# Convolutional window attention on one core: normalisation of queries and keys moved from ScalarE to VectorE, copy of the transposed probabilities moved from VectorE to ScalarE

## The chip, the cores and the metric

The kernel runs on one core of a Trainium2 chip. A core has TensorE (PE), VectorE (DVE), ScalarE (ACT) and GpSimd (POOL), each with its own in-order stream of instructions, a queue for DMA issues on SyncE (SP), and semaphores between them. The metric is the device time of one execution in microseconds (us).

## The reference

The input x is 4 images of 32 channels and 128 by 128 pixels. With gn the normalisation of each channel over its image:

```python
xw = gn(x) cut into 64 windows of 16x16 per image
q, k, v = conv3(xw, qw), conv3(xw, kw), conv3(xw, vw)   # 3x3, then 2x2 pixels into channels:
q, k, v = ln(q), ln(k), ln(v)                            # 64 tokens x 128 features per window, normalised over features
attn = softmax(q @ k.T * SCALE + bias)                   # 8 heads of 16
out  = (attn @ v) @ proj_w.T + proj_b
xr   = xw + out, put back into the image
y    = xr + conv3(gelu(conv3(xr, c1w)), c2w)
return x + y
```

## The kernel before

**Tiling.** Two windows are one pair: 128 tokens on the 128 partitions. An image has 32 pairs. A software pipeline runs over a step number i from -4 to 35; in step i every engine works on other pairs at once. The order on each engine is written out by hand in a function `step` per engine, and every dependence is a semaphore count (`wait_ge`, `then_inc`), so nothing is reordered. Eight steps form a loop body that runs twice; four images run one after the other. Around the change, one step holds:

- TensorE: the query, key and value convolutions of pair i+4 into `y_ps` (L999, L1004), every fourth step the projection into `ox_ps` (L1020), the transposes of queries and keys of pair i+3 into `t_ps` (L1029), the scores of pair i into `s_ps` (L1051), the transpose of the probabilities of pair i-1 into `pt_ps` (L1062, waits for `exped`), the product with the values of pair i-2 into `o_ps` (L1072, waits for `pt_copied`), and one transpose of the output (L986).
- VectorE: statistics of pair i+4 (L547 to L552), scores plus bias `sc` (L558), every fourth step the addition to `xr` (L567), the row maximum `mx` (L573), the copy of `pt_ps` to `pt` (L579), in some steps two memsets of `xnf` (L509, L510), reciprocal `rs` and normalised output `on` of pair i-2 (L587, L593, wait for `pv_done`, the end of L1072).
- GpSimd: the scale `ln_rs` and shift `ln_nr` of the normalisation of pair i+4 (L719 to L726), the subtraction of the maximum from `sc` (L731), the low half `x_lo` of the split input (L701).
- ScalarE: in some steps `xnf` (L766) and the high half `x_hi` (L774), in even steps the affine of queries and keys `q_m`, `k_m` (L816, L820), every fourth step four copies `ot` (L832), then the normalisation of queries and keys of pair i+4 `qk_n` (L845), that of the values `v_bd` (L853), and exp of `sc` of pair i (L861).

I number steps by i modulo 4: the four copies `ot` come in steps 2; L1020, L567, `xnf` and its memsets in steps 3.

**Around the pipeline.** From step 28 on, tiles of the first output convolution (`c1`, L975) take the place of the attention convolutions. The tiles of the second (`c2`, L1094) follow, and the last four of them lie between the steps -4 to -1 of the next image (`head`); there VectorE works off each tile with two instructions in `result` (L609, L614), put behind its own step.

Of the kernel before, what the change touches and what calls it, by code (L numbers as in the profile page):

```python
# [10 lines left out]
ALU = mybir.AluOpType  # L11
# [43 lines left out]
def conv_attention(nc, x_al, x_sh, wqkv, bqkv, bias_t, proj_t, vecs, w1, w2, ident, sel_mean, sel_ones, out):  # L55
    with ExitStack() as ctx:
# [239 lines left out]
        def has(n):  # L296
            return 0 <= n < PAIRS
# [64 lines left out]
        def _(v):  # L362
# [176 lines left out]
            def step(i, p0, h0, r0, rr0, row0, b=None, followed=False):  # L539

                if has(i + 4):
                    m = i + 4
                    v.wait_ge(conv_done, p0 + (m + 1))
                    if m >= 2:
                        v.wait_ge(ln_scales, p0 + (m - 1))
                    for t in range(3):
                        ins = v.bn_stats(ln_st[m % 2][:, t, :], y_ps[m % 2][:, E * t:E * (t + 1)])  # L547
                    ins.then_inc(ln_stats, 1)
                    v.wait_ge(ln_stats, p0 + (m + 1))
                    v.tensor_copy(wait_slot[:, :], vec[:, 0:1])  # L550
                    for t in range(3):
                        ins = v.bn_aggr(ln_mv[m % 2][:, t, :], ln_st[m % 2][:, t, :])  # L552
                    ins.then_inc(ln_moments, 1)
                if has(i):
                    v.wait_ge(scores_done, p0 + (i + 1))
                    if i >= 4:
                        v.wait_ge(ptr_done, p0 + (i - 3))
                    v.tensor_tensor(sc[i % 4][:, :, :, :].rearrange("p (a h) w k -> p a (h w k)", a=2),  # L558
                                    s_ps[:, :, 0:256], biasS[:, :, :], ALU.add).then_inc(biased, 1)

                if i % 4 == 3 and i >= 7:
                    r = (i - 7) // 4
                    v.wait_ge(proj_done, r0 + (r + 1))
                    if i == 7:
                        v.wait_ge(xr_begun, b * 4 + 5)
                    rows = xr[:, bass.ds((row0 + r) * TS, TS), :].rearrange("p i (w j) -> p w i j", w=NWIN)
                    v.tensor_tensor(rows, rows, ox_ps[:, :].rearrange("p (w i j) -> p w i j", w=NWIN, i=TS),  # L567
                                    ALU.add).then_inc(xr_added, 1)
                if has(i):
                    v.wait_ge(biased, p0 + (i + 1))  # L570
                    if i >= 2:
                        v.wait_ge(shifted, p0 + (i - 1))
                    v.tensor_reduce(mx[i % 2][:, :, :], sc[i % 4][:, :, :, :], AX.X, ALU.max).then_inc(maxed, 1)  # L573
                if has(i - 1):
                    m = i - 1
                    v.wait_ge(ptr_done, p0 + (m + 1))
                    if m >= 2:
                        v.wait_ge(pv_done, p0 + (m - 1))
                    v.tensor_copy(pt[m % 2][:, :, :], pt_ps[:, :, :]).then_inc(pt_copied, 1)  # L579

                if i % 4 == 3 and 2 <= (i + 9) // 4 < NROW:
                    row((i + 9) // 4, r0)

                if has(i - 2):
                    m = i - 2
                    v.wait_ge(pv_done, p0 + (m + 1))
                    v.reciprocal(rs[m % 2][:, :, :], o_ps[:, :, :, VW - 1]).then_inc(sums_inv, 1)  # L587
                    v.wait_ge(sums_inv, p0 + (m + 1))
                    if m >= 2:
                        v.wait_ge(ot_done, p0 + (m - 1))  # L590
                    for par in range(2):
                        q = slice(64 * par, 64 * par + 64)
                        ins = v.tensor_tensor(  # L593
                            on[m % 2][q, :, :, :],
                            o_ps[q, :, :, HD * par:HD * (par + 1)].rearrange("p h w d -> p w h d"),
                            rs[m % 2][q, :, :].rearrange("p h w -> p w h").unsqueeze(3).to_broadcast(
                                [64, 2, HP, HD]),
                            ALU.mult)
                    ins.then_inc(normed, 1)

                if PAIRS - 4 <= i < PAIRS and followed:
                    for j in range(2):
                        stats(b + 1, 2 * (i - (PAIRS - 4)) + j)
                for t in low_in.get(i, ()):
                    low(b, t)
# [146 lines left out]
        def _(act):  # L752
# [49 lines left out]
            def step(i, p0, h0, r0, rr0, row0, b=None, followed=False):  # L802
# [7 lines left out]
                if i % 2 == 0 and has(i + 2):  # L810
# [10 lines left out]
                                             ACT.Identity, scale=k_aff[:, par, 0:1], bias=k_aff[:, par, 1:2])  # L821
                    ins.then_inc(qkt_done, 1)

                if i % 4 == 2 and i >= 6:
                    r = (i - 6) // 4
                    act.wait_ge(ot_done, p0 + (4 * r + 4))
                    if r >= 2:
                        act.wait_ge(proj_done, r0 + (r - 1))

                    for w in range(2):  # L830
                        for par in range(2):
                            ins = act.activation(  # L832
                                ot[r % 2][64 * par:64 * par + 64, :].rearrange("p (m w t) -> p m w t", w=2, t=TOK)[:, :, w, :],
                                ox_ps[64 * w:64 * w + 64, :].rearrange("p (m a t) -> p m a t", a=2, t=TOK)[:, :, par, :],
                                ACT.Copy)
                    ins.then_inc(ot_copied, 1)

                if has(i + 4):
                    m = i + 4
                    j = m % 2  # L840
                    act.wait_ge(ln_scales, p0 + (m + 1))
                    if m >= 2:
                        act.wait_ge(tr_done, p0 + (m - 1))
                    for t in range(2):
                        ins = act.activation(qk_n[j][:, t, :].rearrange("p (h y x) -> p h y x", h=HEADS, y=2),  # L845
                                             by_head(y_ps[j][:, E * t:E * (t + 1)]), ACT.Identity,
                                             scale=ln_rs[j][:, t:t + 1], bias=ln_nr[j][:, t:t + 1])
                    ins.then_inc(ln_qk, 1)
                    if m >= 8:
                        act.wait_ge(pv_done, p0 + (m - 7))  # L850
                    for w in range(2):
                        q = slice(64 * w, 64 * w + 64)
                        ins = act.activation(  # L853
                            v_bd[m % 8][q, :, w, 0:2 * HD].rearrange("p h (a y x) -> p h a y x", a=2, y=2),
                            y_ps[j][q, 2 * E:3 * E].rearrange("p (y h a x) -> p h a y x", y=2, h=HP, a=2),
                            ACT.Identity,
                            scale=ln_rs[j][q, 2:3], bias=ln_nr[j][q, 2:3])
                    ins.then_inc(ln_v, 1)
# [375 lines left out]
```

## Time and profile before

| | |
|---|---|
| median of 3 runs | 892.53 us (889.89 to 893.34) |
| profiled execution: time, span | 889.67 us, 887.2 us |
| busy: PE, DVE, ACT, POOL | 86%, 75%, 75%, 57% of the span |
| mean granted TensorE clock | 0.976 of full |

Busy time is the union of an engine's instructions. The profile's averages mix the pipeline's steps with the stages of the two output convolutions, so that a stretch has to be looked at by itself.

### The profile page before, as it was taken

The page shows a single profiled execution, that of the slowest core. Times are in us where ns is not written, and L with a number is a line of the kernel's source. Part 1 is how long each engine was busy: PE and PEld are TensorE (multiplying, and loading weights), DVE is VectorE, ACT ScalarE, POOL GpSimd, SP SyncE. Part 2 cuts the span into 40 slices and gives each one's busy share as a digit, 9 for nine tenths or more (in the row PEclk, how much of TensorE's full clock was granted, in tenths as well). Part 3 has the DMA queues.
Part 4 walks back from the last instruction along what each step waited for, and adds up shares of the span by engine and source line. Part 5 has one row for each costly group of instructions (what it writes and reads, how often), then busy time and mean ns, then how long its engine had stood idle before and what let it go on. Part 6 is the DMA issues. An engine that isn't in the chain of part 4 may idle for free.

```text
span 887.2 us, 19085 instructions
## 1 busy us (share of the span) xinstructions
PE 767.0 (86%) x5704; PEld 540.5 (61%) x5704; DVE 666.9 (75%) x2142; ACT 664.6 (75%) x1351; POOL 506.1 (57%) x857
## 2 busy tenths in 40 slices
PE   0479999999798999999877999998988899999988
PEld 0256776766356777677534767776734576776753
DVE  6557888878656888887675788887876688887575
ACT  1499999765577999976458999986665899997561
POOL 5558777662426777754153777676242667775510
PEclk9989999999998999999999999999998999999999
DMA  6100032000232130300042013020014112000004
GB/s 240 54 28 28 29 121 87 15 1 1 68 121 61 33 118 5 101 1 1 1 155 72 28 29 121 14 88 1 1 54 132 39 54 75 0 1 1 1 1 142
DMA packets 17658, 47.16 MB, mean 53 GB/s; under 512 B 2081, under 2 KB 2721, under 8 KB 17569
## 3 DMA queue, kind: packets, MB, share of 16 engines
q1 hardware_dynamic: 17568, 46.09, 15.9%
q8 instruction: 42, 0.69, 0.3%
q14 instruction: 48, 0.39, 0.1%
HBM read 37.69 MB, written 8.39 MB: 52 GB/s over the span
## 4 chain that ended last, share of the span: by engine, by line
PE 26%; issue 24%; DVE 21%; ACT 16%; POOL 11%; DVEq 1%; DMA 0%; POOLq 0%; SPq 0%; ACTq 0%
PE y_ps L1004 6%; PE s_ps L1094 5%; POOL ln_rs L723 4%; DVE ln_st L547 4%; ACT ot L832 3%; ACT qk_n L845 3%; PE s_ps L1051 3%; PE o_ps L1072 3%; ACT v_bd L853 3%; PE ox_ps L1020 3%; ACT sc L861 2%; ACT q_m L816 2%; PE y_ps L975 2%; PE pt_ps L1062 2%; DVE h_hi L516 2%
## 5 line engine op out<-in xcount | busy, mean ns | idle before, releaser
L845 ACT ACTIVATE qk_n<-y_ps,ln_nr,ln_rs 128x128 f32<-128x128 f32 x256 | 103.3, 455 | 69.0 <-POOL ln_nr L726 67.8
L1004 PE MATMUL y_ps<-w_hi,x_hi 128*128 128x192 f16 (+1 forms) x512 | 151.1, 295 | 0.0
L1004 PE MATMUL y_ps<-w_lo,x_hi 128*128 128x192 f16 (+1 forms) x512 | 150.4, 294 | 0.0
L1004 PE MATMUL y_ps<-w_hi,x_lo 128*128 128x192 f16 (+1 forms) x512 | 150.3, 294 | 0.0
L701 POOL TENSOR_TENSOR x_lo<-xnf,x_hi 128x448 f16<-128x448 f32 (+1 forms) x128 | 140.3, 1112 | 15.1 <-ACT x_hi L774 15.1
L731 POOL TENSOR_TENSOR sc<-sc,mx 128x512 f32<-128x512 f32 x128 | 133.4, 1042 | 22.7 <-DVE mx L573 22.3
L558 DVE TENSOR_TENSOR sc<-s_ps,biasS 128x512 f32<-128x512 f32 x128 | 86.6, 677 | 59.3 <-PE s_ps L1051 57.3
L1072 PE MATMUL o_ps<-v_bd,pt 128*128 128x66 f32 x1024 | 128.6, 268 | 0.0
L547 DVE BATCH_NORM_STATS2 ln_st<-y_ps 128x6 f32<-128x128 f32 x384 | 88.8, 287 | 52.2 <-PE y_ps L1004 44.9
L1072 PEld LDWEIGHTS o_ps<-v_bd,pt 128*128 128x128 f32 x1024 | 124.5, 192 | 0.2
L723 POOL TENSOR_TENSOR ln_rs<-ln_ve,neg_half 128x3 f32<-128x3 f32 x128 | 112.8, 881 | 10.7
L853 ACT ACTIVATE v_bd<-y_ps,ln_nr,ln_rs 64x128 f32<-64x128 f32 x256 | 115.7, 452 | 1.7
L719 POOL TENSOR_TENSOR ln_ve<-ln_mv,eps_y 128x3 f32<-128x3 f32 x128 | 24.6, 192 | 159.8 <-DVE ln_mv L552 158.0
L1062 PE MATMUL pt_ps<-idf,sc 128*128 128x128 f32 x512 | 85.2, 290 | 18.7 <-ACT sc L861 18.4
L861 ACT ACTIVATE sc<-sc 128x512 f32<-128x512 f32 x128 | 80.6, 630 | 26.3 <-POOL sc L731 23.5
L1051 PE MATMUL s_ps<-k_m,q_m 64*128 64x128 f32 x1024 | 93.3, 300 | 1.0 <-issue 0.8
L708 POOL TENSOR_TENSOR xr_lo<-xr,xr_hi 128x512 f16<-128x512 f32 x32 | 36.4, 1138 | 99.7 <-ACT xr_hi L793 99.7
L573 DVE TENSOR_REDUCE mx<-sc 128x8 f32<-128x512 f32 x128 | 87.6, 685 | 4.4
L579 DVE COPY pt<-pt_ps 128x512 f32<-128x512 f32 x128 | 87.2, 681 | 4.5 <-PE pt_ps L1062 4.5
L1051 PEld LDWEIGHTS s_ps<-k_m,q_m 64*128 64x128 f32 x1024 | 68.5, 188 | 26.2 <-issue 26.2
L593 DVE TENSOR_TENSOR on<-o_ps,rs 64x128 f32<-64x128 f32 x256 | 73.9, 289 | 6.2
L1062 PEld LDWEIGHTS pt_ps<-idf,sc 128*128 128x128 f32 x512 | 54.6, 142 | 38.5 <-ACT sc L861 29.4
(160 smaller groups left out, 1619.7 us busy)
## 6 DMA issues: line engine op xcount, KB each, us to landing
xs<-in_x_sh_dram SPq DMA_DIRECT2D x32, 576.0 KB, 3.9
xst<-in_x_al_dram SPq DMA_DIRECT2D x16, 512.0 KB, 7.2
xf<-in_x_al_dram SPq DMA_DIRECT2D x32, 256.0 KB, 4.2
out_dram<-xf SPq DMA_DIRECT2D x32, 256.0 KB, 2.3
wst<-in_wqkv_dram SPq DMA_DIRECT2D x1, 768.0 KB, 3.7
w1s<-in_w_dram SPq DMA_DIRECT2D x1, 256.0 KB, 8.8
w2s<-in_w_dram SPq DMA_DIRECT2D x1, 256.0 KB, 8.8
biasS<-in_bias_t_dram SPq DMA_DIRECT2D x1, 256.0 KB, 9.5
```

Source lines behind the costliest of these rows:

```text
L547: ins = v.bn_stats(ln_st[m % 2][:, t, :], y_ps[m % 2][:, E * t:E * (t + 1)])
L573: v.tensor_reduce(mx[i % 2][:, :, :], sc[i % 4][:, :, :, :], AX.X, ALU.max).then_inc(maxed, 1)
L701: pool.tensor_tensor(at_offset(x_lo[r % 2], a), rows_under(xnf[r % 2], a), at_offset(x_hi[r % 2], a), ALU.subtract).then_inc(xlo_done, 1)
L723: pool.tensor_tensor(ln_rs[j][:, :], ln_ve[j][:, :], neg_half[:, 0:3], ALU.pow).then_inc(ln_pow, 1)
L731: pool.tensor_tensor(sc[i % 4][:, :, :, :], sc[i % 4][:, :, :, :], mx[i % 2][:, :, :].unsqueeze(3).to_broadcast([P, HP, 2, TOK]), ALU.subt ...
L845: ins = act.activation(qk_n[j][:, t, :].rearrange("p (h y x) -> p h y x", h=HEADS, y=2), by_head(y_ps[j][:, E * t:E * (t + 1)]), ACT.Identity,
L853: ins = act.activation(v_bd[m % 8][q, :, w, 0:2 * HD].rearrange("p h (a y x) -> p h a y x", a=2, y=2), y_ps[j][q, 2 * E:3 * E].rearrange(" ...
L861: act.activation(sc[i % 4][:, :, :, :], sc[i % 4][:, :, :, :], ACT.Exp).then_inc(exped, 1)
L1004: ins = pe.matmul(y.rearrange("p (t e) -> p t e", t=3)[:, :, cols], xx[r % 2][:, a, P * s:P * (s + 1)], ww[:, a, :].rearrange("p (t e) -> ...
L1051: ins = pe.matmul(out[:, :, w, :], q_m[h % 2][rows, 2 * (i % 2) + w, :, :].rearrange("p a t -> p (a t)"), k_m[h % 2][rows, :, tok], start= ...
L1062: ins = pe.transpose(pt_ps[:, g, :], sc[m % 4][:, g, :, :].rearrange("p w k -> p (w k)"), idf[:, :])
L1072: ins = pe.matmul(o_ps[:, g, :, :].rearrange("p w d -> p (w d)"), pt[m % 2][:, g, :], v_bd[m % 8][:, g, :, :].rearrange("p w d -> p (w d)" ...
```

## The change

The copy `pt` leaves VectorE and becomes an ACTIVATE Copy on ScalarE, put behind `q_m` and `k_m` and ahead of `ot`. The two `qk_n` instructions leave ScalarE and become tensor_scalar instructions with two per-partition operands on VectorE, put at the end of its step, behind `on`. ScalarE's wait ahead of `v_bd` is now on `ln_qk`, which VectorE raises.

```diff
@@ VectorE, step
                     v.tensor_reduce(mx[i % 2][:, :, :], sc[i % 4][:, :, :, :], AX.X, ALU.max).then_inc(maxed, 1)
-                if has(i - 1):
-                    m = i - 1
-                    v.wait_ge(ptr_done, p0 + (m + 1))
-                    if m >= 2:
-                        v.wait_ge(pv_done, p0 + (m - 1))
-                    v.tensor_copy(pt[m % 2][:, :, :], pt_ps[:, :, :]).then_inc(pt_copied, 1)
-
...
                     ins.then_inc(normed, 1)
 
+                if has(i + 4):
+                    m = i + 4
+                    j = m % 2
+                    v.wait_ge(ln_scales, p0 + (m + 1))
+                    if m >= 2:
+                        v.wait_ge(tr_done, p0 + (m - 1))
+                    for t in range(2):
+                        ins = v.tensor_scalar(qk_n[j][:, t, :].rearrange("p (h y x) -> p h y x", h=HEADS, y=2),
+                                              by_head(y_ps[j][:, E * t:E * (t + 1)]), ln_rs[j][:, t:t + 1],
+                                              ln_nr[j][:, t:t + 1], ALU.mult, ALU.add)
+                    ins.then_inc(ln_qk, 1)
@@ ScalarE, step
                     ins.then_inc(qkt_done, 1)
 
+                if has(i - 1):
+                    m = i - 1
+                    act.wait_ge(ptr_done, p0 + (m + 1))
+                    if m >= 2:
+                        act.wait_ge(pv_done, p0 + (m - 1))
+                    act.activation(pt[m % 2][:, :, :], pt_ps[:, :, :], ACT.Copy).then_inc(pt_copied, 1)
+
...
                     act.wait_ge(ln_scales, p0 + (m + 1))
-                    if m >= 2:
-                        act.wait_ge(tr_done, p0 + (m - 1))
-                    for t in range(2):
-                        ins = act.activation(qk_n[j][:, t, :].rearrange("p (h y x) -> p h y x", h=HEADS, y=2),
-                                             by_head(y_ps[j][:, E * t:E * (t + 1)]), ACT.Identity,
-                                             scale=ln_rs[j][:, t:t + 1], bias=ln_nr[j][:, t:t + 1])
-                    ins.then_inc(ln_qk, 1)
+                    act.wait_ge(ln_qk, p0 + (m + 1))
```

The rows below are ScalarE's instructions from `x_hi` of a step 2 to exp of the same step, before the change; `REGISTER_ALU` prepares a count to wait for.

```order
L774 ACTIVATE x_hi<-xnf 128x8x56
L816 ACTIVATE q_m<-t_ps,q_aff 128x4x64 x2
L820 ACTIVATE k_m<-t_ps,k_aff 128x256 x2
L832 ACTIVATE ot<-ox_ps 64x4x64 x4
L841 REGISTER_ALU
L845 ACTIVATE qk_n<-y_ps,ln_nr,ln_rs 128x128 x2
L850 REGISTER_ALU
L853 ACTIVATE v_bd<-y_ps,ln_nr,ln_rs 64x4x32 x2
L861 ACTIVATE sc<-sc 128x512
```

The same place of the changed kernel:

```order
L779 ACTIVATE x_hi<-xnf 128x8x56
L821 ACTIVATE q_m<-t_ps,q_aff 128x4x64 x2
L825 ACTIVATE k_m<-t_ps,k_aff 128x256 x2
L834 ACTIVATE pt<-pt_ps 128x512
L844 ACTIVATE ot<-ox_ps 64x4x64 x4
L853 REGISTER_ALU
L859 ACTIVATE v_bd<-y_ps,ln_nr,ln_rs 64x4x32 x2
L866 REGISTER_ALU
L867 ACTIVATE sc<-sc 128x512
```

One instruction of 512 elements a partition stands where the four copies begin, and two of 128 are gone ahead of `v_bd`.

The next rows are VectorE's step 3 of the first group of an image (where L567 is still absent), before the change.

```order
L547 BN_STATS ln_st<-y_ps 128x6 x3
L550 COPY wait_slot<-vec 128x1
L552 BN_AGGR ln_mv<-ln_st 128x2 x3
L558 TENSOR_TENSOR sc<-s_ps,biasS 128x512
L573 TENSOR_REDUCE mx<-sc 128x8
L579 COPY pt<-pt_ps 128x512
L507 ISA
L509 MEMSET xnf 32x8x16
L510 MEMSET xnf 32x8x16
L587 RECIPROCAL rs<-o_ps 128x8
L593 TENSOR_TENSOR on<-o_ps,rs 64x128 x2
```

The same step of the changed kernel:

```order
L547 BN_STATS ln_st<-y_ps 128x6 x3
L550 COPY wait_slot<-vec 128x1
L552 BN_AGGR ln_mv<-ln_st 128x2 x3
L558 TENSOR_TENSOR sc<-s_ps,biasS 128x512
L573 TENSOR_REDUCE mx<-sc 128x8
L507 ISA
L509 MEMSET xnf 32x8x16
L510 MEMSET xnf 32x8x16
L580 RECIPROCAL rs<-o_ps 128x8
L586 TENSOR_TENSOR on<-o_ps,rs 64x128 x2
L601 TENSOR_SCALAR qk_n<-y_ps,ln_rs,ln_nr 128x128 x2
```

The copy is gone from the middle, and `qk_n` is the last thing in the step, behind `on`.

## Rows read from the trace of the kernel before

**Rows 1.** The page: busy time, share of the span and instructions per engine.

```profile
PE 767.0 (86%) x5704; PEld 540.5 (61%) x5704; DVE 666.9 (75%) x2142; ACT 664.6 (75%) x1351; POOL 506.1 (57%) x857
```

**Rows 2.** Windows: length, busy PE, PEld, DVE, ACT, POOL, granted clock, DMA share, GB/s.

```profile
300.15:356.65 56.50, 52.96 (x438) 40.34 (x439) 46.68 (x165) 52.18 (x112) 42.03 (x73) 1.00 0.18 59
```

**Rows 3.** Timeline of ScalarE: start, duration, instructions, [idle before and its releaser].

```profile
323.12 0.92 ACT L853 ACTIVATE v_bd<-y_ps,ln_nr,ln_rs 64x128 f32<-64x128 f32 x2
324.06 0.63 ACT L861 ACTIVATE sc<-sc 128x512 f32<-128x512 f32 x1
...
327.94 0.81 ACT L845 ACTIVATE qk_n<-y_ps,ln_nr,ln_rs 128x128 f32<-128x128 f32 x2 [0.81 <-POOL ln_nr L726]
...
331.70 0.81 ACT L845 ACTIVATE qk_n<-y_ps,ln_nr,ln_rs 128x128 f32<-128x128 f32 x2 [0.45 <-POOL ln_nr L726]
...
333.88 0.56 ACT L774 ACTIVATE x_hi<-xnf 128x448 f16<-128x448 f32 x1
...
336.28 1.54 ACT L832 ACTIVATE ot<-ox_ps 64x256 f32<-64x256 f32 x4
337.85 0.81 ACT L845 ACTIVATE qk_n<-y_ps,ln_nr,ln_rs 128x128 f32<-128x128 f32 x2
...
341.38 0.81 ACT L845 ACTIVATE qk_n<-y_ps,ln_nr,ln_rs 128x128 f32<-128x128 f32 x2
```

**Rows 4.** Timeline of a step 3: the projection on PE, then VectorE.

```profile
318.92 1.13 PE L1020 MATMUL ox_ps<-ot,projg 128*128 128x512 f32 x2 [0.33 <-ACT ot L832]
...
320.95 0.69 DVE L558 TENSOR_TENSOR sc<-s_ps,biasS 128x512 f32<-128x512 f32 x1 [1.22 <-PE s_ps L1051]
...
322.15 0.68 DVE L573 TENSOR_REDUCE mx<-sc 128x8 f32<-128x512 f32 x1
...
323.50 0.17 DVE L509 MEMSET xnf<- 32x128 f32 x1
...
324.02 0.21 DVE L587 RECIPROCAL rs<-o_ps 128x8 f32<-128x8 f32 x1
324.27 0.59 DVE L593 TENSOR_TENSOR on<-o_ps,rs 64x128 f32<-64x128 f32 x2
324.93 0.69 DVE L547 BATCH_NORM_STATS2 ln_st<-y_ps 128x6 f32<-128x128 f32 x3
```

**Rows 5.** Timeline of PE: transpose of the probabilities, product with the values.

```profile
340.17 0.66 PE L1062 MATMUL pt_ps<-idf,sc 128*128 128x128 f32 x4 [0.31 <-ACT sc L861]
340.67 1.00 PE L1072 MATMUL o_ps<-v_bd,pt 128*128 128x66 f32 x8
```

**Rows 6.** Groups by line: busy us, mean ns, idle before.

```profile
L547 DVE BATCH_NORM_STATS2 ln_st<-y_ps 128x6 f32<-128x128 f32 x384 | 88.8, 287 | 52.2 <-PE y_ps L1004 44.9 <-issue 4.8
L579 DVE COPY pt<-pt_ps 128x512 f32<-128x512 f32 x128 | 87.2, 681 | 4.5 <-PE pt_ps L1062 4.5
L845 ACT ACTIVATE qk_n<-y_ps,ln_nr,ln_rs 128x128 f32<-128x128 f32 x256 | 103.3, 455 | 69.0 <-POOL ln_nr L726 67.8
L832 ACT ACTIVATE ot<-ox_ps 64x256 f32<-64x256 f32 x128 | 48.3, 377 | 15.9 <-PE ox_ps L986 14.8
L456 DVE TENSOR_SCALAR pbias<-pt_ps,vec,up 128x1 f32<-128x1 f32 x1 | 0.3, 273 | 0.0
```

**Rows 7.** Timeline of ScalarE: `qk_n` in step 2 and in step 26 of an image.

```profile
280.63 0.81 ACT L845 ACTIVATE qk_n<-y_ps,ln_nr,ln_rs 128x128 f32<-128x128 f32 x2 [0.34 <-POOL ln_nr L726]
...
394.18 0.81 ACT L845 ACTIVATE qk_n<-y_ps,ln_nr,ln_rs 128x128 f32<-128x128 f32 x2
```

**Rows 8.** Timeline of a step of the head: GpSimd's last normalisation instruction, VectorE's `result`.

```profile
252.76 0.19 POOL L726 TENSOR_TENSOR ln_nr<-ln_nm,ln_rs 128x3 f32<-128x3 f32 x1
252.99 0.75 DVE L609 SCALAR_TENSOR_TENSOR yt<-s_ps,c_scale,xr 128x512 f32<-128x512 f32 x1 [1.75 <-PE s_ps L1094]
```

**Rows 9.** Timeline of PE behind its longest wait of that stretch.

```profile
271.65 0.68 PE L1029 MATMUL t_ps<-idf,qk_n 128*128 128x128 f32 x2 [3.14 <-ACT qk_n L845]
...
273.42 1.11 PE L1062 MATMUL pt_ps<-idf,sc 128*128 128x128 f32 x4
```

## Prediction

> **What bounds the kernel now.** I first read the busy shares [rows 1]: no engine is full, so the average says nothing and I went to a stretch of the pipeline. Over three groups of four steps, 56.50 us, PE is busy 52.96 and ScalarE 52.18 us at full clock [rows 2]: a group takes 18.83 us, of which PE needs 17.65 and ScalarE 17.39. Then I read ScalarE's timeline. The starts of `qk_n` at 327.94 (a step 0), 331.70, 337.85 and 341.38 give 3.76 us to step 1, 6.15 to step 2, 3.53 to step 3 and, as the group is 18.83, 5.39 to the next step 0 [rows 3]. ScalarE waits 0.81 and 0.45 us per group for GpSimd's `ln_nr`, and else runs through [rows 3]. So ScalarE bounds the kernel, PE 7% behind it. What matters for the change is that the short steps make up for the long one: while ScalarE works on step 2, the other engines go ahead, and the next steps cost less than 4 us.
>
> **What the change adds and removes.**
>
> ScalarE loses two `qk_n`, 0.81 us as a pair [rows 3]; since they overlap by 0.10 (2 x 0.455 against 0.81) [rows 3, 6], the next instruction comes 0.70 earlier. It gains one Copy of 512 elements from PSUM. From below: `ot`, the same function from PSUM for half the elements, 0.377 [rows 6]. From above: twice that, 0.754. Exp has the copy's length and, like it, no per-partition operands: 0.63 [rows 3]. I take 0.60, near exp, which it is most like. Less the overlap, and with 0.02 for its wait, it adds 0.52. ScalarE's own work falls by about 0.2 us a step. Taken alone, that is a gain.
>
> VectorE loses a copy of 681 ns, worth 0.60 in its queue: L573 starts at 322.15, and without the copy the memset could start at 322.90 in place of 323.50 [rows 4, 6]. It gains two tensor_scalar instructions of 128 elements from PSUM with two per-partition operands. The trace has no such row. From below: a statistics instruction of 128 elements from PSUM without such operands, 287 ns. From above: one with two such operands and 1 element, 273 ns [rows 6], all of it fixed, plus 127 elements at what the copy pays per element at most (681/512 = 1.33 ns), 169: 442 ns. I take 0.405, near the top, because the 1-element row has the same operands and everything it takes is fixed; the statistics row less its fixed share gives some 0.13 for the elements. As a pair, less an overlap of 0.08 (three statistics instructions of 0.287 take 0.69 [rows 4, 6]), 0.73. VectorE's work grows by 0.1 us a step; it is busy 46.68 of 56.50 us, 17% idle [rows 2], so this is not the cost.
>
> A rule would make it cheaper. The Trainium skill ("VectorE: DVE Perf Modes", The TRN2 errata) gives 120 cycles plus one per element at 0.96 GHz for VectorE from PSUM: 258 ns for 128, a pair 0.44. By it the forecast below would be 21 us lower (0.29 in 18 steps of each image). For the copy it gives 658 against 681 in the trace, but its fixed share is 125 ns, and the row with two operands has 273. The rows decide.
>
> **The cost is the order.** Now `v_bd` of a pair waits for `qk_n` on VectorE; `qk_n` stands behind `on` of an earlier pair, which waits for L1072; L1072 stands behind L1062, which waits for exp; and exp stands behind `v_bd` on ScalarE. That is a closed ring once per step: queued behind the waiting `v_bd` is exp, and for it wait PE, then VectorE, then ScalarE again. Its links: `v_bd` start to exp start 0.94, exp 0.63 [rows 3]; to L1062 0.05 (taken), from its start to the start of L1072 0.50, L1072 1.00 [rows 5]; to `rs` 0.05 (taken); `rs` start to `on` end 0.84; to the next instruction 0.07 [rows 4]; `qk_n` 0.73; to ScalarE 0.03 (taken from the gap between 337.82 and 337.85 [rows 3]). Sum 4.84 us. The steps of 3.76 and 3.53 us are no longer possible.
>
> Let V be the start of `v_bd` in a step.
> - Step 0 to 1, and 3 to 0: the ring, 4.84 each. In step 0, ScalarE's own work (1.57 for `v_bd` and exp, `x_hi`, four affines, copy) is 1.57 + 2.40 (333.88 to 336.28) + 0.52 = 4.5 [rows 3], hidden.
> - Step 1 to 2: ScalarE's own queue. 6.15 less 0.70 plus 0.52 = 5.97. The ring is shorter and hidden.
> - Step 2 to 3: L1020 waits for `ot`, which ends at V (L1020 at 318.92). From there 2.03 us to L558, through L567, L573, memsets, `rs` and `on` to 324.86, 5.94 us [rows 4]; less 0.60 for the copy, plus 0.07 and `qk_n` 0.73, plus 0.03: 6.17. On this path VectorE was hidden before, because `qk_n` did not wait for it.
>
> A group: 4.84 + 4.84 + 5.97 + 6.17 = 21.82 against 18.83, +2.99 us.
>
> Per image: step 6 to 22 are four such groups, +12.0. The first, from step 2 at 280.63 to step 6 at about 300.1 (the window of [rows 2] begins with the L1020 behind that step), 19.5 us, is without L567 and so without the long step 3: 3 x 4.84 + 5.97 = 20.5, +1.0. The last ends at 394.18 and begins at 300.1 and four groups of 18.83, 375.4 [rows 2, 7]: 18.8 us. It has L567 but no memsets, so its step 3 is 6.17 less about 0.65 (0.52 from the first memset to `rs` and the gap ahead [rows 4]); with two rings and 5.97 it is 21.2, +2.4. The steps on either side I put at +0.8, one late `qk_n`. Sum 16.2, times 4: 64.8 us.
>
> In the head, VectorE now waits for GpSimd inside its step, ahead of `result`. `ln_nr` ends at 252.95, so `qk_n` runs to 253.7, and `result` starts there and not at 252.99, 0.7 later [rows 8]. VectorE was idle for 1.75 there; with 0.7 more per step over it, it becomes the bound. About 1.6 us per head (three steps, less what the last hides), 3 heads: 5.
>
> At steps 28 to 32 there is no `qk_n`, VectorE loses 0.60 a step and PE has the `c1` tiles. If VectorE alone bounds there, 5 steps of 4 images give 12 us back; if PE does, nothing. I count nothing, since ScalarE's copy comes into the way from `pt_ps` to `o_ps`, and keep the 12 for the range.
>
> Sum: 64.8 + 5 = 70 us. On the profiled time of 889.67 that is 960; the median of the runs shown is 2.86 higher, so **962 us**, 7.9% slower.
>
> **The rivals.**
>
> *Only the long places cost.* If PE were ready early and the ring of the light steps had shorter links (`qk_n` as a pair 0.5, no gaps), the two ring steps would be near PE's own (17.65 - 1.13) / 4 = 4.1 [rows 2, 4], and a group 4.1 + 4.1 + 5.97 + 5.94 = 20.1, +1.3: 24 groups and the heads, 36 us, 929 us. For it: a sum of ten links, three of them taken (0.13 us). Against: each other link is in the rows.
>
> *Faster.* ScalarE bounds the kernel and gets lighter. If `qk_n` were always ready when ScalarE comes to `v_bd`, PE would be the bound with 17.65 a group, 1.18 less, 24 groups: 28 us, 864 us. It decides at the point at which step 2 to 3 and the two rings together cost 3.0 us less than I sum, so that the group is 18.83 again; that is a full microsecond off each. It would need `qk_n` to be done before `on`, which the order of VectorE's instructions excludes.
>
> *No change.* The ring just about fills the slack: 21.82 less 3.0 by errors of several links. Same point; 892 us.
>
> *The clock falls.* After an idle time of 3.14 us, PE's L1062 took 1.11 us in place of 0.66 [rows 9, 5], the lower of the two levels (1.2 for 2.4 GHz). With the change PE is busy 17.65 of 21.82 us; the 4.2 idle lie in four steps, about 1 us each. If that sufficed to put a third of a step's 4.4 us of work at the lower level in each group, +1.5 us in each of 24 groups, 36 us: 998 us. That takes an idle time of about 1 us to do what 3.14 did, and I think it unlikely. The Trainium skill ("TensorE: Matmul & The Clock Gate", What's actually happening) also has the clock fall after idle time; by that rule, the row agrees.
>
> **How the numbers follow.** Forecast 0.63, only the long places 0.14, clock 0.09, faster 0.09, no change 0.05. The forecast's own range is 940 to 985: `qk_n` from 0.49 to 0.80 as a pair in three of four steps (-19 to +6 us over 80 steps), latencies of 0.1 us in as many (8 us), ScalarE's copy at 0.38 to 0.75 us in 24 steps (5 and 4 us), the 12 us of steps 28 to 32. To hold 8 in 10 it reaches into both neighbours: 922 to 995. Half a per cent is about what a measurement of this kernel can tell from no change: faster 0.09, same 0.05, slower 0.86.
>
> **What would show it.** Right: ScalarE waits ahead of `v_bd`, put down to VectorE's `qk_n`, in steps 3, 0 and 1 and not in 2; PE waits for exp ahead of L1062 by about 0.5 us more in each of these; the four-step group is near 21.8, ScalarE near 75% busy in it; the pair `qk_n` 0.73, the copy 0.59 us; granted clock 1.00 there; `result` in the head 0.7 later. Wrong: a group below 18.8, or ScalarE without waits ahead of `v_bd`; a group that is long because PE's matmuls are; or time that goes to steps 28 and later.

## The result and the profile after

| | before | after |
|---|---|---|
| median | 892.93 us (889.89 to 896.02, 4 runs) | 969.84 us (968.82 to 970.42, 4 runs) |
| profiled execution: time, span, clock | 889.67, 887.2, 0.976 | 970.42, 968.6, 0.971 |

The ratio is 1.086 (95% interval 1.0821 to 1.0899): 8.6% slower. The forecast of 962 us was 8 us low, and the time lies in the narrower of the two ranges stated with it (940 to 985 us).

The page's busy shares, to be held against [rows 1], with the pair of groups for the two moved operations against [rows 6]:

```profile
PE 784.5 (81%) x5704; PEld 548.2 (57%) x5704; DVE 691.5 (71%) x2270; ACT 647.0 (67%) x1223; POOL 508.4 (52%) x857
```

Groups by line (busy us, mean ns, idle before):

```profile
L601 DVE TENSOR_SCALAR qk_n<-y_ps,ln_rs,ln_nr 128x128 f32<-128x128 f32 x256 | 93.3, 406 | 31.8 <-POOL ln_nr L731 28.5
L834 ACT ACTIVATE pt<-pt_ps 128x512 f32<-128x512 f32 x128 | 77.0, 601 | 20.5 <-PE pt_ps L1068 18.9
```

ScalarE has 17.6 us less work than before and VectorE 24.6 us more, and neither number explains 77 us. The window of one group (length, busy PE, PEld, DVE, ACT, POOL, clock, DMA share, GB/s), against [rows 2]:

```profile
330.93:352.78 21.85, 18.10 (x147) 13.51 (x147) 16.51 (x60) 16.80 (x33) 14.24 (x24) 1.00 0.10 29
```

A group that took 18.83 us takes 21.85, at full clock, and no engine is busy for more than 83% of it. ScalarE was at 92%, now it is at 77%. What bounds the kernel now is a chain of waits that closes on itself (the ring of the prediction), as the rows below and then the experiments show. ScalarE's timeline of the same group shows where it stands still (start, duration, [idle before and releaser]), against [rows 3]:

```profile
330.93 0.93 ACT L859 ACTIVATE v_bd<-y_ps,ln_nr,ln_rs 64x128 f32<-64x128 f32 x2 [2.77 <-issue]
...
335.78 0.93 ACT L859 ACTIVATE v_bd<-y_ps,ln_nr,ln_rs 64x128 f32<-64x128 f32 x2 [0.35 <-issue]
336.73 0.63 ACT L867 ACTIVATE sc<-sc 128x512 f32<-128x512 f32 x1
...
340.63 0.93 ACT L859 ACTIVATE v_bd<-y_ps,ln_nr,ln_rs 64x128 f32<-64x128 f32 x2 [1.61 <-issue]
...
345.00 1.55 ACT L844 ACTIVATE ot<-ox_ps 64x256 f32<-64x256 f32 x4
346.57 0.93 ACT L859 ACTIVATE v_bd<-y_ps,ln_nr,ln_rs 64x128 f32<-64x128 f32 x2
...
352.78 0.46 ACT L859 ACTIVATE v_bd<-y_ps,ln_nr,ln_rs 64x128 f32<-64x128 f32 x1 [2.77 <-issue]
```

`v_bd` waits in step 3 (330.93), 0, 1 and again 3, and not in step 2 (346.57), where the four `ot` copies lie ahead of it. The releaser reads "issue" or `qk_n`, as the profile puts it down; that it is `qk_n` each time is seen from VectorE's rows, which end just before (below, the one at 339.81 ends at 340.54, `v_bd` starts at 340.63). The steps are 4.85, 4.85, 5.94 and 6.21. The rest of the ring in step 0 to 1, on PE and VectorE:

```profile
337.41 0.66 PE L1068 MATMUL pt_ps<-idf,sc 128*128 128x128 f32 x4 [0.51 <-ACT sc L867]
337.90 1.00 PE L1078 MATMUL o_ps<-v_bd,pt 128*128 128x66 f32 x8
...
338.95 0.21 DVE L580 RECIPROCAL rs<-o_ps 128x8 f32<-128x8 f32 x1 [0.58 <-PE o_ps L1078]
339.19 0.59 DVE L586 TENSOR_TENSOR on<-o_ps,rs 64x128 f32<-64x128 f32 x2
339.81 0.73 DVE L601 TENSOR_SCALAR qk_n<-y_ps,ln_rs,ln_nr 128x128 f32<-128x128 f32 x2
...
346.60 1.13 PE L1026 MATMUL ox_ps<-ot,projg 128*128 128x512 f32 x2 [1.08 <-ACT ot L844]
...
348.63 0.69 DVE L558 TENSOR_TENSOR sc<-s_ps,biasS 128x512 f32<-128x512 f32 x1 [1.98 <-PE s_ps L1057]
```

From `v_bd` at 335.78: 0.95 to exp, 0.68 to L1068, 0.49 to L1078, 1.05 to `rs`, 0.86 to `qk_n`, 0.82 to the next `v_bd` at 340.63: 4.85. The last two rows are the long step: `ot` releases L1026 at 346.60, and VectorE's queue from 348.63 on ends with `qk_n`, which releases `v_bd` at 352.78. The waits over the whole run say the same (who waited for what: us in total, times, longest):

```profile
ACT v_bd L859 <- issue: 81.9, 47, 2.8
ACT v_bd L859 <- DVE qk_n L601: 74.8, 54, 3.0
DVE rs L580 <- PE o_ps L1078: 55.6, 79, 3.6
PE pt_ps L1068 <- ACT sc L867: 44.3, 80, 0.9
PE t_ps L1035 <- DVE qk_n L601: 43.5, 39, 5.5
```

Each neighbour in the ring waits for the one ahead of it; in the kernel before the third of these rows had 0.2 us, the fourth 18.4.

**Where the 80.75 us between the two profiled executions lie** (970.42 - 889.67), by the starts of `v_bd` in the 32 steps of each image:

| stretch | forecast, 4 images | measured | per image |
|---|---|---|---|
| steps 6 to 22, four groups | 48 | 55.3 | 14.7, 13.3, 14.8, 12.4 |
| steps 2 to 6 | 4 | 7.0 | 2.2, 1.5, 1.7, 1.6 |
| steps 22 to 26 | 9.6 | 10.1 | 2.5 each |
| all else: head, edges, steps 27 and later | 8.2 | 8.4 | |

The 12.4 of image 4 are groups without disturbance. Images 1, 2 and 3 hold five steps (two, one and two) in which PE ran at the lower of its two clock levels (1.2 for 2.4 GHz), as these rows of PE in image 1 show:

```profile
112.78 1.12 PE L1026 MATMUL ox_ps<-ot,projg 128*128 128x512 f32 x2 [1.08 <-ACT ot L844]
...
118.94 0.44 PE L1035 MATMUL t_ps<-idf,qk_n 128*128 128x128 f32 x2 [1.10 <-DVE qk_n L601]
...
120.68 1.09 PE L1068 MATMUL pt_ps<-idf,sc 128*128 128x128 f32 x4 [0.54 <-ACT sc L867]
121.57 1.81 PE L1078 MATMUL o_ps<-v_bd,pt 128*128 128x66 f32 x8
```

L1068 takes 1.09 us in place of 0.66 and L1078 1.81 in place of 1.00, behind waits of 1.10 and 0.54 us. L1068 and L1078 are links of the ring, so two steps there took 6.20 and 6.09 us in place of 5.00 and 4.85. DMA traffic was high in this place (the DMA engines were busy all the time from 120 to 126), but is not the cause: in image 3 the clock (the third number from the end) was at the lower level with no DMA at all (the second):

```profile
608.82:615.00 6.18, 6.18 (x28) 4.89 (x28) 2.48 (x8) 4.53 (x10) 2.97 (x4) 0.50 0.00 0
```

### The profile page after: what moved, and what is told of

Same layout as the page of the kernel before. It is cut to its first block, busy times and chain, and to the rows that moved or that the text cites. A ratio compares the mean times of both kernels' runs of the same rounds, so it can differ in the third digit from the quotient of the medians.

```text
span 968.6 us, 19193 instructions
## 1 busy us (share of the span) xinstructions
PE 784.5 (81%) x5704; PEld 548.2 (57%) x5704; DVE 691.5 (71%) x2270; ACT 647.0 (67%) x1223; POOL 508.4 (52%) x857
## 4 chain that ended last, share of the span: by engine, by line
issue 31%; PE 27%; DVE 19%; ACT 14%; POOL 7%; DVEq 1%; ACTq 0%; DMA 0%; SPq 0%; POOLq 0%
PE o_ps L1078 7%; PE pt_ps L1068 5%; ACT sc L867 5%; ACT v_bd L859 4%; DVE qk_n L601 4%; PE ox_ps L1026 3%; PE s_ps L1057 3%; POOL ln_rs L728 3%; PE y_ps L1010 2%; PE y_ps L981 2%; ACT ot L844 2%; PE s_ps L1100 2%; DVE yt L614 2%; DVE ln_st L547 2%; DVE h_hi L516 2%
## 5 line engine op out<-in xcount | busy, mean ns | idle before, releaser
L1078 PE MATMUL o_ps<-v_bd,pt 128*128 128x66 f32 x1024 | 131.1, 272 | 0.0
L1078 PEld LDWEIGHTS o_ps<-v_bd,pt 128*128 128x128 f32 x1024 | 127.1, 195 | 0.2
L1068 PE MATMUL pt_ps<-idf,sc 128*128 128x128 f32 x512 | 86.3, 293 | 44.4 <-ACT sc L867 44.3
L601 DVE TENSOR_SCALAR qk_n<-y_ps,ln_rs,ln_nr 128x128 f32<-128x128 f32 x256 | 93.3, 406 | 31.8 <-POOL ln_nr L731 28.5
L1068 PEld LDWEIGHTS pt_ps<-idf,sc 128*128 128x128 f32 x512 | 55.5, 144 | 65.4 <-ACT sc L867 52.3
L1035 PE MATMUL t_ps<-idf,qk_n 128*128 128x128 f32 x256 | 55.5, 299 | 44.7 <-DVE qk_n L601 43.5
L834 ACT ACTIVATE pt<-pt_ps 128x512 f32<-128x512 f32 x128 | 77.0, 601 | 20.5 <-PE pt_ps L1068 18.9
```

Of the source, the lines that this page charges most:

```text
L601: ins = v.tensor_scalar(qk_n[j][:, t, :].rearrange("p (h y x) -> p h y x", h=HEADS, y=2), by_head(y_ps[j][:, E * t:E * (t + 1)]), ln_rs[j] ...
L1068: ins = pe.transpose(pt_ps[:, g, :], sc[m % 4][:, g, :, :].rearrange("p w k -> p (w k)"), idf[:, :])
L1078: ins = pe.matmul(o_ps[:, g, :, :].rearrange("p w d -> p (w d)"), pt[m % 2][:, g, :], v_bd[m % 8][:, g, :, :].rearrange("p w d -> p (w d)" ...
```

## The experiments

All times stand beside the kernel before on the same chip: 891.4 us for the two halves and the two single reorderings, 891.2 for both reorderings, `qk_n` twice, PE's waits filled and `ot` split, 894.3 for the copy twice and for before with exp first. The copy twice, `ot` split and before with exp first are medians of four runs; the other seven have one run each. The kernel before and the kernel after spread by 6.1 and 1.6 us over their four runs, so differences between single runs of a few us say little by themselves. The table gives the time between starts of `v_bd`, the median of each kind of step in the steps 6 to 22 of four images, and the mean length of a group. For the kernel after, 3 to 0 is 4.85 inside a loop body and 5.0 where one begins or ends (4.85 at the end in image 4).

| kernel | us | 3 to 0 | 0 to 1 | 1 to 2 | 2 to 3 | mean group | clock |
|---|---|---|---|---|---|---|---|
| before | 892.9 | 5.34 | 3.76 | 6.14 | 3.53 | 18.83 | 0.976 |
| after | 969.8 | 5.00 | 4.85 | 5.94 | 6.21 | 22.28 | 0.971 |
| only `qk_n` moved | 990.1 | 5.36 | 5.21 | 5.46 | 6.81 | 23.29 | 0.952 |
| only the copy moved | 909.1 | 5.04 | 3.83 | 6.62 | 4.01 | 19.50 | 0.979 |
| after, `qk_n` ahead of `rs` | 922.3 | 5.06 | 4.34 | 5.94 | 4.66 | 20.05 | 0.970 |
| after, exp ahead of `v_bd` | 928.1 | 4.36 | 4.42 | 6.05 | 5.55 | 20.43 | 0.980 |
| both reorderings | 933.5 | 4.81 | 4.37 | 6.06 | 4.98 | 20.54 | 0.966 |
| after, `qk_n` twice | 1033.9 | 5.63 | 5.48 | 5.93 | 6.84 | 24.00 | 0.963 |
| after, copy twice | 986.7 | 4.92 | 4.85 | 6.41 | 6.21 | 22.71 | 0.973 |
| after, PE's waits filled | 964.1 | 4.86 | 4.85 | 5.94 | 6.21 | 21.92 | 0.977 |
| before, `ot` split | 897.9 | 5.97 | 3.75 | 5.36 | 4.04 | 19.13 | 0.977 |
| before, exp first | 1007.8 | 5.20 | 5.28 | 6.29 | 5.75 | 22.68 | 0.966 |

### One half at a time

The first kernel is the changed one with the copy back on VectorE, the second the changed one with `qk_n` back on ScalarE. In short, from after:

```diff
@@ e1_qk_only: VectorE, behind mx
+                if has(i - 1):
...
+                    v.tensor_copy(pt[m % 2][:, :, :], pt_ps[:, :, :]).then_inc(pt_copied, 1)
@@ ScalarE
-                if has(i - 1):
...
-                    act.activation(pt[m % 2][:, :, :], pt_ps[:, :, :], ACT.Copy).then_inc(pt_copied, 1)
```

```diff
@@ e2_copy_only: VectorE, end of step
-                        ins = v.tensor_scalar(qk_n[j][:, t, :].rearrange("p (h y x) -> p h y x", h=HEADS, y=2),
...
@@ ScalarE, ahead of v_bd
-                    act.wait_ge(ln_qk, p0 + (m + 1))
...
+                        ins = act.activation(qk_n[j][:, t, :].rearrange("p (h y x) -> p h y x", h=HEADS, y=2),
+                                             by_head(y_ps[j][:, E * t:E * (t + 1)]), ACT.Identity,
+                                             scale=ln_rs[j][:, t:t + 1], bias=ln_nr[j][:, t:t + 1])
```

> Only the normalisation of queries and keys is on VectorE, behind the normalised output; the copy of the transposed probabilities stays on VectorE. Ring theory: the ring v_bd, exp, transpose, product, normalised output, qk_n is untouched by where the copy is, so two steps stay at 4.85 to 4.95 us; step 1 to 2 falls to 5.45 (ScalarE without the copy), step 2 to 3 rises to 6.8 (VectorE with it): group about 22.0 us, time 965 to 980 us, mid 972. Rival (the cost of the change is ScalarE's copy, which puts exp and the values later): without it the group falls to about 20 us and the time to 930 us or less.

> Only the copy of the transposed probabilities is on ScalarE; the normalisation of queries and keys stays there too. Ring theory: no ring, but ScalarE, which bounds the kernel, gets 0.52 us more per step, 2.08 per group, of which its waits of 1.26 for GpSimd take up a part: group 19.5 to 20.7 us, time 905 to 938 us, mid 919. The two halves then do not add up to the whole (about 80 and 27 against 77). Rival (the copy is what costs): the time is within 15 us of the changed kernel, 955 us or more.

Measured: 990.08 and 909.13. The move of `qk_n` alone makes the ring and costs more than the whole change; the copy alone costs 18 us. In its undisturbed groups the first kernel shows 4.85, 4.84, 5.46 and 6.81, which is 21.96 as said. It is 10 us above its expected range since it has many more steps at the lower clock. PE in one of them, its long wait in step 3 to 0 and what came behind:

```profile
360.45 0.44 PE L1035 MATMUL t_ps<-idf,qk_n 128*128 128x128 f32 x2 [1.70 <-DVE qk_n L608]
...
360.93 1.08 PE L1057 MATMUL s_ps<-k_m,q_m 64*128 64x128 f32 x8
362.19 1.11 PE L1068 MATMUL pt_ps<-idf,sc 128*128 128x128 f32 x4 [0.18 <-ACT sc L867]
```

The two kernels give ScalarE's two terms apart: step 1 to 2 goes from 6.14 to 5.46 without `qk_n` (0.68; the working had 0.70), and from 6.14 to 6.62 with the copy (0.48; it had 0.52). Both together are 5.94, which is what after shows. VectorE's copy costs 0.60 in step 2 to 3 (6.81 against 6.21), as taken.

### Opening the ring by order

If the ring is what costs, the same instructions in another order must give most of it back. One kernel puts `qk_n` directly behind the row maximum, so that it no longer stands behind `on`; the other puts exp ahead of `v_bd`, so that exp no longer stands behind the wait for `qk_n`; the third does both.

```diff
@@ e3_qk_ahead: VectorE, step
                     v.tensor_reduce(mx[i % 2][:, :, :], sc[i % 4][:, :, :, :], AX.X, ALU.max).then_inc(maxed, 1)
+                    for t in range(2):
+                        ins = v.tensor_scalar(qk_n[j][:, t, :].rearrange("p (h y x) -> p h y x", h=HEADS, y=2),
...
                 if i % 4 == 3 and 2 <= (i + 9) // 4 < NROW:
                     row((i + 9) // 4, r0)
...
-                    for t in range(2):
-                        ins = v.tensor_scalar(qk_n[j][:, t, :].rearrange("p (h y x) -> p h y x", h=HEADS, y=2),
@@ e4_exp_first: ScalarE, step, ahead of v_bd
+                if has(i):
+                    act.wait_ge(shifted, p0 + (i + 1))
+                    act.activation(sc[i % 4][:, :, :, :], sc[i % 4][:, :, :, :], ACT.Exp).then_inc(exped, 1)
...
-                if has(i):
-                    act.wait_ge(shifted, p0 + (i + 1))
-                    act.activation(sc[i % 4][:, :, :, :], sc[i % 4][:, :, :, :], ACT.Exp).then_inc(exped, 1)
```

> The changed kernel with qk_n on VectorE moved ahead of the xnf memsets, reciprocal and normalised output, directly behind the row maximum. Nothing else. Ring theory: qk_n no longer waits for the product with the values, the ring is open; what is left is VectorE's own queue (statistics 1.1, wait for GpSimd's scales 1.74, qk_n 0.75, output 0.87: 4.45 us a step), ScalarE's step 1 to 2 of 5.95, step 2 to 3 of 4.75 and step 3 to 0 of 5.15: group about 20.3 us, time 915 to 940 us, mid 928. Rival (VectorE's instructions with two per-partition operands, or its load, are the cost, wherever they stand): the time stays above 960 us.

> The changed kernel with exp put ahead of v_bd on ScalarE; qk_n stays at the end of VectorE's step. Ring theory: exp no longer stands behind the waiting v_bd, so the ring is open at another place; the next one is product, normalised output, qk_n, transposes, scores, transpose of the probabilities, about 4.3 us. Step 2 to 3 keeps its 6.2, step 1 to 2 falls to 5.4: group about 20.1 us, time 915 to 945 us, mid 930. Rival (what costs is that qk_n itself comes late, for the transposes behind it): the time stays above 960 us.

> Both orders changed: qk_n directly behind the row maximum on VectorE, and exp ahead of v_bd on ScalarE. If each only opened the same ring, the second adds little: group 19.4 to 20.0 us, time 905 to 922 us. If ScalarE's step 1 to 2 (5.94 to 6.05) and step 2 to 3 are what is left, the group stays above the 18.83 of the kernel before, and so does the time, by 1% or more. Rival (the two delays are independent and add): 885 us or less.

Measured: 922.31, 928.08 and 933.52. Each single reordering takes back 40 to 48 of the 77 us without moving a single operation to another engine. In the first, `qk_n` stands ahead of `rs`, and the ring steps are shorter. VectorE and ScalarE of its step 3 to 0:

```profile
334.58 0.72 DVE L581 TENSOR_SCALAR qk_n<-y_ps,ln_rs,ln_nr 128x128 f32<-128x128 f32 x2
335.38 0.92 ACT L859 ACTIVATE v_bd<-y_ps,ln_nr,ln_rs 64x128 f32<-64x128 f32 x2 [1.23 <-issue]
...
335.90 0.21 DVE L592 RECIPROCAL rs<-o_ps 128x8 f32<-128x8 f32 x1
```

In the second, the time came as expected and two of the steps did not: step 1 to 2 was to fall to 5.4 and is 6.05, step 2 to 3 was to keep 6.2 and is 5.55. Exp now stands between `ot` and `v_bd`, so step 1 to 2 still holds it, and the long path from `ot` has only its last 5.55 us behind `v_bd`.

That both together give more, which I expected (905 to 922), is refuted: they are slower than the first alone. With exp ahead, `v_bd` comes later in step 2 to 3 (4.98 against 4.66), since exp waits for GpSimd's subtraction, and PE waits longer for `ot`, as it comes to L1025 earlier:

```profile
356.97 1.12 PE L1025 MATMUL ox_ps<-ot,projg 128*128 128x512 f32 x2 [1.92 <-ACT ot L844]
...
362.05 0.63 ACT L852 ACTIVATE sc<-sc 128x512 f32<-128x512 f32 x1 [1.52 <-POOL sc L736]
```

Three steps 2 to 3 are at the lower clock (6.50, 6.52 and 6.40 in place of 4.98). Of the 11 us by which both together are slower than the first, these are 4.5, the order in the groups of steps 6 to 22 is about 3 (an undisturbed group is 20.21 against 20.01); the rest lies outside those groups and was not taken apart.

### Doubling one operation

```diff
@@ e5_qk_twice: VectorE, end of step
+                    for t in range(2):
+                        v.tensor_scalar(qk_x[j][:, t, :].rearrange("p (h y x) -> p h y x", h=HEADS, y=2),
+                                        by_head(y_ps[j][:, E * t:E * (t + 1)]), ln_rs[j][:, t:t + 1],
+                                        ln_nr[j][:, t:t + 1], ALU.mult, ALU.add)
@@ e6_copy_twice: ScalarE
+                    act.activation(pt_x[m % 2][:, :, :], pt_ps[:, :, :], ACT.Copy)
```

> The changed kernel with the two qk_n instructions issued twice on VectorE, once into a tile that nobody reads; 0.65 us more per step there. Ring theory: every step that the ring or VectorE's queue decides gets 0.65 us more (3 to 0 and 0 to 1: 4.85 to 5.5; 2 to 3: 6.21 to 6.86), step 1 to 2 stays at 5.94, since ScalarE's queue decides it and the ring, 5.5, is below: group plus 1.95, four images with 18 such steps each plus 47 us, head and edges plus 8: 1025 us, 1015 to 1040 with more or fewer stretches at the lower clock. Rival (VectorE has a quarter of its time idle, its load hides): within 10 us of the changed kernel, 960 to 980.

> The changed kernel with the copy of the transposed probabilities issued twice on ScalarE, the first time into a tile that nobody reads: 0.52 us more in ScalarE's queue per step. My account of the changed kernel: the copy is not a link of the ring, so the step 1 to 2 (ScalarE's own queue) grows from 5.94 to 6.46, the step 3 to 0, whose ScalarE queue I put at 4.5 us, from 4.85 to about 5.0, and 0 to 1 and 2 to 3 stay; the group goes from 21.85 to 22.5, and the time from 970 to 986 us (979 to 994). Rival: ScalarE's load is paid in every step, 2.1 us a group: 1020 us or more. Rival: the copy is hidden everywhere: 970 us.

Measured: 1033.92, and 986.72 (985.70 to 988.57; ratio to before 1.1052, 1.1007 to 1.1096). A second pair on VectorE is 0.63 to 0.65 in its queue, and exactly the three steps that pass through `qk_n` grow by it: 4.85 to 5.48, 4.85 to 5.48 and 6.21 to 6.84. The step 1 to 2 does not move. A second copy on ScalarE does the reverse: only step 1 to 2 grows, 5.94 to 6.41. Step 3 to 0 stays at 4.85 inside a loop body and 5.0 at its edges, where I had expected it to grow to about 5.0; the median of 4.92 lies between the two, and the steps above 5.0 are again at the lower clock. ScalarE around that step:

```profile
349.30 0.61 ACT L835 ACTIVATE pt_x<-pt_ps 128x512 f32<-128x512 f32 x1
349.78 0.62 ACT L836 ACTIVATE pt<-pt_ps 128x512 f32<-128x512 f32 x1
350.25 1.55 ACT L846 ACTIVATE ot<-ox_ps 64x256 f32<-64x256 f32 x4
351.83 0.92 ACT L861 ACTIVATE v_bd<-y_ps,ln_nr,ln_rs 64x128 f32<-64x128 f32 x2
```

The second instruction moves what follows by 0.48 (349.30 to 349.78), and `v_bd` at 351.83 has no wait to hide it. The two kernels tell the links of the ring from the work beside it.

### The clock

```diff
@@ e8_pe_warm: TensorE, ahead of L1026 in steps 3 and ahead of L1035 in steps 0, for 4 <= i < 28
+                    pe.wait_ge(biased, p0 + i)
+                    for d in range(8):
+                        pe.matmul(s_ps[:, 0, 256:512], w_hi[:, 0, 0:P], w_lo[:, 0, 0:256], start=True, stop=True)
```

> The changed kernel with eight f16 matmuls of 256 columns, 0.86 us, from constants into unused columns of s_ps in each of PE's two longest waits of a group (ahead of L1020 in step 3, ahead of the transposes in step 0), steps 4 to 27. If the single steps of 6.1 us in place of 4.85 come from the lower clock, and this from PE's waits, they vanish: all steps 3 to 0 and 0 to 1 of the middle groups at 4.85 to 5.0, time 960 to 965 us. Rival (they come from elsewhere, or the added matmuls delay PE): the same number of such steps, or 970 us and more.

Measured: 964.09. PE gets work that nobody reads in its two longest waits of a group, and in the steps 6 to 22 none is left that is longer than its kind is at full clock. The group is 21.92 on average against 22.28. A group's window:

```profile
330.00:352.00 22.00, 19.90 (x164) 15.02 (x162) 16.51 (x59) 16.96 (x34) 14.30 (x26) 1.00 0.11 29
```

PE has 1.8 us more to do in a group than in the changed kernel and the kernel is 5.8 us faster. So the clock is worth about 6 us of the 77, and order and queues the rest. That is one run, and counted from the kernel before on its own chip (72.9 us against 76.9) it is 4; the groups themselves, 0.36 us each in 16, give 6.

### Was there a gain in the kernel before?

If ScalarE bounded the kernel before, taking work from its longest step must help. The first kernel does that without touching `qk_n`: two of the four `ot` copies go to VectorE, behind `on`. The second, the kernel before with the same edit of exp as above (ahead of `qk_n` and `v_bd`), is the control for that reordering.

```diff
@@ e7_split_ot (on before): ScalarE, steps 2
-                    for w in range(2):
+                    for w in range(1):
@@ VectorE, steps 2, behind on
...
+                    for par in range(2):
+                        ins = v.tensor_copy(
+                            ot[r % 2][64 * par:64 * par + 64, :].rearrange("p (m w t) -> p m w t", w=2, t=TOK)[:, :, 1, :],
+                            ox_ps[64:128, :].rearrange("p (m a t) -> p m a t", a=2, t=TOK)[:, :, par, :])
...
@@ TensorE, ahead of L1020
-                    pe.wait_ge(ot_copied, r0 + (r + 1))
+                    pe.wait_ge(ot_copied, r0 * 2 + (2 * r + 2))
```

> The kernel before with two of the four ot copies of each step 2 (those of the second window, 64 partitions x 256 elements) on VectorE, behind its normalised output; ScalarE keeps the other two. Nothing waits on ScalarE for VectorE, so no ring arises. If ScalarE bounds the kernel before, step 1 to 2 falls from 6.14 by 0.77 and a group to 18.0 to 18.3 us, time 872 to 882 us (PE's own work of 17.65 a group is the floor, 864 us). Rival (the slack is already full elsewhere: VectorE's later statistics or the later L1020): within 0.5% of before or slower.

> The kernel before with one edit: exp of a pair stands ahead of the normalisations of queries, keys and values on ScalarE instead of behind them. It is the control of the reordering that gained in the changed kernel. If the gain there came only from the ring that the change closed, nothing is to be had here: 885 to 900 us, or slower where exp waits for GpSimd's subtraction and holds the normalisations up, 900 to 920 us. Rival: an early exp is worth as much without the ring as with it (1.5 us a group), 850 to 860 us.

Measured: 897.89 (897.82 to 900.19; ratio 1.0083, 1.0065 to 1.0102) and 1007.82 (1004.95 to 1010.05; ratio 1.1281, 1.123 to 1.1332). Both are misses.

In the first, step 1 to 2 fell by 0.78 as said, and the neighbours took 1.1 back: VectorE's copies delay its statistics, these GpSimd's scale and shift, and these ScalarE. Its waits:

```profile
ACT qk_n L856 <- POOL ln_nr L737: 77.4, 90, 3.4
ACT sc L872 <- POOL sc L742: 40.8, 36, 4.3
PE ox_ps L1031 <- DVE ot L607: 21.7, 32, 0.7
```

In before the first two are 67.8 and 23.5 us. So "ScalarE bounds the kernel" was half of it. The short steps were as tight on the way through VectorE and GpSimd, and `ot` work taken from ScalarE and given to VectorE behind `on` finds no slack there, though no ring is closed.

The second was expected at 885 to 920 and is the slowest but one of all. Its timeline shows a ring that I had not thought of:

```profile
338.12 0.63 ACT L840 ACTIVATE sc<-sc 128x512 f32<-128x512 f32 x1
...
338.78 0.81 ACT L848 ACTIVATE qk_n<-y_ps,ln_nr,ln_rs 128x128 f32<-128x128 f32 x2
...
339.71 0.43 PE L1028 MATMUL t_ps<-idf,qk_n 128*128 128x128 f32 x2 [0.44 <-ACT qk_n L848]
...
340.08 0.72 PE L1050 MATMUL s_ps<-k_m,q_m 64*128 64x128 f32 x8
...
340.84 0.69 DVE L558 TENSOR_TENSOR sc<-s_ps,biasS 128x512 f32<-128x512 f32 x1 [2.08 <-PE s_ps L1050]
...
342.05 0.68 DVE L573 TENSOR_REDUCE mx<-sc 128x8 f32<-128x512 f32 x1
...
342.80 1.04 POOL L731 TENSOR_TENSOR sc<-sc,mx 128x512 f32<-128x512 f32 x1 [2.08 <-DVE mx L573]
...
343.88 0.63 ACT L840 ACTIVATE sc<-sc 128x512 f32<-128x512 f32 x1 [2.10 <-POOL sc L731]
```

`qk_n` now stands behind exp; PE's transposes wait for it, and the scores stand behind the transposes; the scores lead through VectorE and GpSimd to the next exp. That is 5.76 us from exp to exp, and step 2 to 3 of this kernel takes 5.75. The same move of exp gained about 40 us in the changed kernel, where `qk_n` is not in ScalarE's queue. This reading comes from the rows of one step; no kernel took this second ring away, so it is argued and not shown.

## Why the prediction was right, point by point

- **The ring.** Forecast 4.84 us with ten links, measured 4.85 in 14 of the 16 steps 0 to 1 between steps 6 and 22 and in 7 of the 16 steps 3 to 0; of the others, 6 are the 5.0 at the edges of a loop body, which the sum did not have, and 5 are at the lower clock. Doubling `qk_n` shows that it is a link; the two reorderings show the links from `on` to `qk_n` and from `v_bd` to exp. Those through PE were read from rows and not varied. Two small links were off and cancel: `on` to `qk_n` 0.03 for 0.07, `qk_n` to `v_bd` 0.09 for 0.03.
- **Step 1 to 2, ScalarE's queue.** 5.97 against 5.94; the copy was 601 ns (0.60 forecast), in the queue 0.48 (0.52). The second copy shows that this is the one step where ScalarE's work counts in full.
- **Step 2 to 3.** 6.17 against 6.21.
- **Price of `qk_n` on VectorE.** 405 forecast from two rows of other instructions, 406 measured, 0.73 as a pair, as forecast. The estimate of 258 ns from the rule of the Trainium skill ("VectorE: DVE Perf Modes", The TRN2 errata) did not hold for an instruction with two per-partition operands; by the doubled kernel, whose three steps grew by 0.63 and not by 0.44, it does not hold in the queue either.
- **The copy on ScalarE.** The Trainium skill ("ScalarE: Activation LUTs", What ACT_TABLE_LOAD costs) has 186 ns and 0.833 per element for an instruction without per-partition operands, which makes an estimate of 613 for 512. Here the trace, with 601, agrees.
- **Steps 28 and later.** Nothing was counted, and the 12 us kept for the range did not come back. Instead the way from the last `v_bd` of an image to the first of the next grew by 0.9 us (62.5 to 63.4), 2.7 over three images. With the copy alone on ScalarE it is 63.2, with `qk_n` alone moved 62.6: it is mostly the copy, a term that the sum put at nothing.
- **First group and head.** Two terms of the sum were mis-sized, in opposite directions. The first group was put at +1.0 and is +1.5 to +2.2: its steps are 5.22 and 5.0 where I wrote the bare ring of 4.84. The heads were put at 1.6 each, and from step -4 to step 0 the three cost 1.0, 1.2 and 0.05. `result` was put 0.7 later behind `ln_nr` and is 0.64 later, but the step grew only from 4.49 to 4.95.
- **The clock, as a rival.** It was priced at 36 us, and dismissed because "that takes an idle time of about 1 us to do what 3.14 did". That sentence failed: the clock fell behind waits of 1.10 and 0.54 us in some groups, and behind one of 1.70 in many of the first experiment's. The sign "granted clock 1.00 there" held in 13 of 16 groups. Its size was 6 us, so the sum stayed near. It is, with the first group, most of what was missing: 80.75 measured against 70 is 10.75, of which the clock is about 7 (steps that stand out in the table of stretches: 2.3, 0.9 and 2.4 over image 4's 12.4, and about 1.5 in the step 1 to 2 of image 4, 7.25 us long where the filled kernel has 5.74; the filled kernel as a whole says 4 to 6), the first groups are 3.0; the rest is the steps 3 to 0 of 5.0 us at the edges of a loop body and the way between images, less what the heads did not cost.
- **PE waits for exp.** Forecast about 0.5 more in three steps. It is 0.47 to 0.58 in these, in place of 0.31 [rows 5], so 0.2 more: I took the total for the increase.
- **The rival "faster".** It rested on ScalarE as the bound. Its condition, `qk_n` ready when ScalarE comes to `v_bd`, is met with both reorderings: between the steps 6 and 22 `v_bd` never waits for `qk_n` there. Still an undisturbed group takes 20.21 us and not 17.65, with ScalarE waiting for GpSimd's subtraction instead (1.52 us in the row at 362.05). So the step that the rival had wrong is that ScalarE's work alone bounds the kernel. `ot` split (898) says the same: ScalarE's longest step got 0.78 us shorter, and the kernel was not faster.

## What to carry to other kernels

Where every engine runs its queue in order, moving an instruction gives it the predecessors of its new place: write down what stands ahead of it there, what that waits for, and whether the path comes back to the waiting engine, and sum such a ring over one step before you count busy time. Doubling one instruction into an unused tile shows within one run which steps pass through it: they grow by its price in the queue, and the others do not. The same reordering can break a ring in one kernel and do harm in another: exp ahead of the normalisations gained about 40 us in the one and lost 114 in the other, where the rows show a new ring.

## What the runs showed of the hardware

- **Short waits can lower the clock.** TensorE fell to the lower level in single steps behind waits of 1.1 and 0.5 us, as they recur in each group; with more idle time in step 3 to 0 (1.70 us) it happened far more often (mean clock 0.952), and with the two longest waits filled not in the steps 6 to 22 at all. It is not regular: image 4 had no such step from step 6 to 22, image 2 one, images 1 and 3 two each. The Trainium skill ("TensorE: Matmul & The Clock Gate", What's actually happening) has the clock fall after idle time; these rows agree in that, with PE at work between the waits.
- **Adding work made the kernel faster.** 16 matmuls a group that nobody reads brought 969.8 to 964.1 us (one run; against the kernel before of each, 76.9 to 72.9 us).
- **Per-partition operands cost VectorE about 60 ns each.** 128 elements from PSUM take 287 ns without them [rows 6] and 406 with two, but these are different instructions. The setup of the kernel after has tensor_scalar instructions alike but for the operands, with few occurrences: 1 element from PSUM takes 158 ns without such an operand and 273 with two, and 128 by 128 take 281 with one and 347 with two:

```profile
L489 DVE TENSOR_SCALAR gm<-ox_ps 128x1 f32<-128x1 f32 x4 | 0.6, 158 | 2.1 <-PE ox_ps L959 2.1
L456 DVE TENSOR_SCALAR pbias<-pt_ps,vec,up 128x1 f32<-128x1 f32 x1 | 0.3, 273 | 0.0
L408 DVE TENSOR_SCALAR bst<-bst,cw 128x128 f32<-128x128 f32 x3 | 0.7, 281 | 0.0
L454 DVE TENSOR_SCALAR projg<-projw,vec,up 128x128 f32<-128x128 f32 x1 | 0.3, 347 | 0.0
```

- **Back-to-back instructions overlap.** On VectorE two of 406 ns take 0.73 us, and a further pair adds 0.64; on ScalarE a further copy of 601 ns adds 0.48.
